# Split fp16 products for the MLP and the query, key and value projections of a fused token, attention and expert layer, and a reordered start

## The reference, cut to what matters

```python
def _L0_tok_ref(x, W1, b1, W2, b2):          # 64 images of 3x224x224 as 196 patches of 768
    h = jax.nn.silu(jnp.einsum('blk,kd->bld', patches, W1) + b1)
    return jnp.einsum('bld,de->ble', h, W2) + b2          # 256 columns

def _L0_attn_ref(x, ...):                    # (64, 228, 256), 16 heads of 16
    xn = _rms_norm(x, ln1_w)
    q, k, v = xn @ Wq, xn @ Wk, xn @ Wv      # then q and k are normalised per head
    attn = (jnp.einsum('bqhd,bkhd->bhqk', q, k) + bias) * scale[None, :, None, None]
    attn = jax.nn.softmax(jnp.where(causal, attn, -1000000.0), axis=-1)
    y = jnp.einsum('bhqk,bkhd->bqhd', attn, v) @ Wo + x
    z = _rms_norm(y, ln2_w)
    return jax.nn.relu(z @ W1) @ W2 + y      # hidden width 1024

def _L0_ffn_ref(x, Wr, W1, b1, W2, b2):      # 8 experts, each takes its top 3648 of 14592 tokens
    h = jax.nn.gelu(jnp.einsum('ekd,edh->ekh', X_in, W1) + b1[:, None, :], approximate=False)
    X_e = jnp.einsum('ekh,ehd->ekd', h, W2) + b2[:, None, :]
    return out.at[idx].add(G * X_e)

h = jnp.concatenate([_L0_tok_ref(x), txt], axis=1)
h = h + _L0_attn_ref(_layernorm(h));  h = h + _L0_ffn_ref(_layernorm(h))
```

## Time and profile before

| | us |
|---|---|
| median of 3 runs | 4300.19 (4299.0 to 4302.61) |
| profiled execution, its own time | 4297.36 |
| its span | 4295.6 |
| mean granted TensorE clock in it | 0.968 of full speed |
| start, up to the second pair's `tok2` block | 175.2 |
| first phase after that (31 passes) | 2492.3 |
| last MLP and router | 54.1 |
| second phase | 1574.0 |

### The profile page before, as it was taken

How to read it: one execution, slowest core, us unless ns; L and a number is a source line. 1 busy time by engine, 2 the same in 40 slices (tenths; PEclk the granted TensorE clock), 3 DMA queues, 4 the chain that set the end, 5 groups by cost and what they waited for, 6 DMA issues and landing times. The chain is left out here.

```text
span 4295.6 us, 78024 instructions
## 1 busy us (share of the span) xinstructions
PE 3876.5 (90%) x26650; PEld 2354.5 (55%) x26650; DVE 2403.7 (56%) x4812; ACT 2035.7 (47%) x3375; POOL 1716.9 (40%) x1367
## 2 busy tenths in 40 slices
PE   2699999999999999999999999339999999999998
PEld 1366566566566566566566566235555555555554
DVE  3455555555555555555555555475555555555554
ACT  1344444444444444444444444225665655655565
POOL 1123323323323323323323322016666666666666
PEclk8799999999999999999999999659999999999999
DMA  7412312312312312312312310532323323323322
GB/s 113 87 35 43 49 34 44 49 34 44 49 34 44 49 34 44 49 34 44 49 34 44 49 22 16 143 99 39 63 45 66 63 46 65 65 46 66 46 46 45
DMA packets 302872, 222.26 MB, mean 52 GB/s; under 512 B 111524, under 2 KB 290182, under 8 KB 302710
## 3 DMA queue, kind: packets, MB, share of 16 engines
q1 hardware_dynamic: 183550, 157.86, 19.1%
q0 software_dynamic: 107264, 62.29, 9.3%
q10 hardware_dynamic: 11896, 0.05, 0.2%
HBM read 117.43 MB, written 63.57 MB: 42 GB/s over the span
## 5 line engine op out<-in xcount | busy, mean ns | idle before, releaser
L1382 DVE TENSOR_TENSOR pr<-pr,bias_t 114x684 f32<-114x684 f32 x512 | 485.6, 968 | 166.3 <-ACT pr L1018 161.9
L1729 POOL DMA_INDIRECT out_dram<-contrib,idx_cur x256 | 531.5, 2076 | 104.8 <-issue 78.8
L1558 DVE SCALAR_TENSOR_TENSOR hTs<-hTe,scales,hTs 128x456 f16<-128x456 f32 x514 | 322.4, 686 | 445.5 <-ACT hTs L1132 445.5
L1018 ACT ACTIVATE pr<-SC 114x684 f32<-114x684 f32 x512 | 376.5, 743 | 339.7 <-PE SC L445 339.4
L511 PE MATMUL G<-w2m,hT 128*114 128x256 f32 x2048 | 511.4, 388 | 1.1 <-DVE hy L1354 1.1
L891 PE MATMUL SC<-xgT,ws 128*128 128x456 f16 x2316 | 468.4, 357 | 0.0
L1722 POOL DMA_INDIRECT xg<-xn_rows,idx_cur x264 | 389.9, 1477 | 117.1 <-issue 60.4
L493 PE MATMUL G<-yT,w1m 128*128 128x456 f32 x1024 | 412.2, 551 | 10.6 <-ACT yT L964 10.6
L371 PE MATMUL G<-img,w1t 128*128 128x392 f32 x768 | 343.4, 538 | 68.3 <-DMA b2t<-in_L_tok_b_dram 49.9
L511 PEld LDWEIGHTS G<-w2m,hT 128*114 128x114 f32 x2048 | 339.9, 178 | 75.6 <-ACT hT L1054 15.4
L1660 POOL TENSOR_TENSOR rstd<-mv,ln_eps 114x4 f32<-114x4 f32 x32 | 7.0, 220 | 881.0 <-DVE mv L1255 881.0
(11 more groups left out here) (229 smaller groups left out, 6725.3 us busy)
## 6 DMA issues: line engine op xcount, KB each, us to landing
raw<-in_x_dram SPq DMA_DIRECT2D x192, 196.0 KB, 6.4
img<-turned SPq DMA_DIRECT2D x384, 98.0 KB, 2.8
we<-in_L_ffn_W_dram SPq DMA_DIRECT2D x34, 1024.0 KB, 7.7
out_dram<-hy SPq DMA_DIRECT2D x32, 456.0 KB
xn_rows<-xn SPq DMA_DIRECT2D x32, 456.0 KB
xg<-xn_rows,idx_cur POOLq DMA_INDIRECT x264, 3.8
out_dram<-contrib,idx_cur POOLq DMA_INDIRECT x256, 5.5
bias_by_distance<-pr SPq DMA_DIRECT2D x1, 3241.9 KB, 37.9
```

Of the source, the lines that this page charges most:

```text
L1018: act.activation(pr[g % 4][:, :, :], SC[g % 2][0:T, :, 0:QW], ACT.Exp).then_inc(exp_done, 1)
L1382: dve.tensor_tensor(pr[g % 4][:, :, :], pr[g % 4][:, :, :], bias_t[:, 2 * pair:2 * pair + 2, :], ALU.mult).then_inc(probs_done, 1)
L1558: dve.scalar_tensor_tensor(hTs[:, 1, m, :], hTe[:, m, :], scale_at(scales, 2, e), hTs[:, 0, m, :], ALU.mult, ALU.subtract).then_inc(h_spli ...
L1729: pool.indirect_dma_start(out=out_rows, out_offset=bass.IndirectOffsetOnAxis(ap=idx_cur[k4][:, t:t + 1], axis=0), in_=contrib[k][:, t, :], ...
```

## The change

1. The projections (`wqkv`), `w1` and `w2` become three fp16 products each. The moving and stationary operands are `xh`, `yh`, `hT` (activations) and `wqkv`, `w1m`, `w2m` (weights), each with a high and a low half in the place of the fp32 data. ScalarE writes the high half; VectorE then writes the low half (`xs_low`, `y2_low`, `hid_low`), and only that frees the bank.
2. Weights are scaled by powers of two from their norms: squares on ScalarE, sums by a TensorE product with ones, exponents on VectorE, then the two halves. For the projections this is done before the first pair, for the MLP after the first pair's attention. The scales are undone where projections are read out and in the residual.
3. `w2` pieces: 8 of 16 stand ahead of the first `qkT`, where it was 2; the rest stand in earlier slots. `mlp_out(0)` stands ahead of `masked_probs`.
4. The bias table is written narrower (341 columns of 455) and read back by three loads. The first images are spread after it, and the table is built ahead of the first `qk_norm`. Loads of the expert biases are moved from ScalarE's queue at the start to SyncE's queue later.
5. In the last pair, the final norm is written by VectorE and all relu are on ScalarE.

On VectorE, in a pass (these rows are the last pass, whose order is that of all), before: from the end of the Newton steps (`rn`) to the low parts of the queries and keys (`qkp`).

The diff, cut to its core:

```diff
@@ operands
-        wqkv = s1("wqkv", [128, KC, 3 * D])
+        wqkv = s1("wqkv", [128, 2, KC, 3 * D], F16)
-        w1m = s1("w1m", [128, KC, HID])
-        w2m = s1("w2m", [128, MC, D])
+        w1m = s1("w1m", [128, 2, KC, HID], F16)
+        w2m = s1("w2m", [128, 2, MC, D], F16)
-        hT = s1("hT", [128, MC, W])
+        hT = s1("hT", [128, 2, MC, W], F16)
...
+        PARTS = ((0, 0), (0, 1), (1, 0))
@@ pe_qkv, pe_w1, pe_w2 (one of three)
+            if m == 0:
+                pe.wait_ge(mlp_split, 2)
-                last = pe.matmul(part.g("w1", m)[:, 0:W], w1m[:, c, m * 128:(m + 1) * 128], yT[:, c, :],
-                                 start=c == 0, stop=c == KC - 1)
+                for n, (wp, yp) in enumerate(PARTS):
+                    last = pe.matmul(part.g("w1", m)[:, 0:W], w1m[:, wp, c, m * 128:(m + 1) * 128], yh[:, yp, c, :],
+                                     start=c == 0 and n == 0, stop=c == KC - 1 and n == len(PARTS) - 1)
@@ slots
-        for n, slot in enumerate((0, 1, 4, 4, 5, 6, 7, 8, 9, 10)):
-            SLOTS[slot].append(("w2", range(6 + n, 7 + n)))
+        for n, slot in enumerate((2, 4, 5, 6)):
+            SLOTS[slot].append(("w2", range(12 + n, 13 + n)))
...
-            w2(0)
+            for n in range(0, 8, 2):
+                w2(n)
             pe_qkT(part, j, 0)
-            w2(2)
+            w2(8)
@@ tensor, start
+            pe.wait_ge(qkv_squares, 2)
+            pe.matmul(SC[1][:, 1, 480:482], sum_ones[:, :], w_sums[:, QK_SUM:V_SUM + 1], start=True, stop=True).then_inc(qkv_norms, 1)
...
+            pe.wait_ge(mlp_squares, 3)
+            pe.matmul(SC[1][:, 1, 484:487], sum_ones[:, :], w_sums[:, WO_SUM:W2_SUM + 1], start=True, stop=True).then_inc(mlp_norms, 1)
@@ scalar
             def relu(part, ms):
                 for m in ms:
                     part.wait_filled(act, "w1", m)
-                    act.activation(hT[:, m, :], part.g("w1", m)[:, 0:W], ACT.Relu).then_inc(evacuated[part.bank("w1", m)], 1)
+                    act.activation(hT[:, 0, m, :], part.g("w1", m)[:, 0:W], ACT.Relu).then_inc(hid_high, 1)
...
             exps(part, 0)
+            act.wait_ge(mlp_folded, 1)
+            squares_of(wo[:, :, :], yT[:, :, 0:D], WO_SUM, mlp_squares)
+            squares_of(flat(w1m_raw), words(w1m), W1_SUM, mlp_squares)
+            squares_of(flat(w2m_raw), words(w2m), W2_SUM, mlp_squares)
+            act.wait_ge(mlp_scale, 1)
+            high_weights(w1m[:, 0, :, :], w1m_raw, W1_K, mlp_high)
+            high_weights(w2m[:, 0, :, :], w2m_raw, W2_K, mlp_high)
@@ vector
+            def xs_low(part, j):
+                for c in range(KC):
+                    dve.wait_ge(xs_high, KC * j + (c + 1))
+                    dve.tensor_tensor(xh[:, 1, c, :], part.g("xsT", c)[:, 0:W], xh[:, 0, c, :],
+                                      ALU.subtract).then_inc(evacuated[part.bank("xsT", c)], 1)
+            def hid_low(part, j, ms):
+                for m in ms:
+                    dve.wait_ge(hid_high, MC * j + (m + 1))
+                    dve.scalar_tensor_tensor(hT[:, 1, m, :], part.g("w1", m)[:, 0:W], 0.0, hT[:, 0, m, :],
+                                             ALU.max, ALU.subtract).then_inc(evacuated[part.bank("w1", m)], 1)
...
             def iteration(part, i):
                 front_a(part, i, False)
                 tail(part, i - 1)
                 router_out(i - 2)
-                front_b(part, i)
+                front_xs(i, range(2))
+                y2_low(part, i - 1)
+                front_xs(i, range(2, NT)).then_inc(xs_done, 1)
+                hid_low(part, i - 1, range(EARLY))
+                xs_low(part, i)
+                hid_low(part, i - 1, (EARLY,))
+                front_xa(part, i)
                 qk_norm(part, i)
+                mlp_out(part, i - 1, 0)
                 masked_probs(part, i)
@@ gpsimd
+            pool.wait_ge(mlp_split, 2)
+            pool.memset(xn2, 0.0).then_inc(xn2_done, 1)
```

More of the change, by code:

```diff
@@ L411, in pe_qkv @@
                         for c in range(KC):
-                            last = pe.matmul(part.g(*key)[0:T, half * D:(half + 1) * D], xsT[:, c, t * T:(t + 1) * T],
-                                             wqkv[:, c, 2 * D:], start=c == 0, stop=c == KC - 1)
+                            for n, (wp, xp) in enumerate(PARTS):
+                                last = pe.matmul(part.g(*key)[0:T, half * D:(half + 1) * D], xh[:, xp, c, t * T:(t + 1) * T],
+                                                 wqkv[:, wp, c, 2 * D:],
+                                                 start=c == 0 and n == 0, stop=c == KC - 1 and n == len(PARTS) - 1)
                 pe_block(part, key, last)
@@ L735, in _ @@
             load_text(1)
+            with nc.allow_non_contiguous_dma(reason="small vectors of weights"):
+                for e in range(NE):
+                    sp.dma_start(fb1c[:, e, :], fb1[e].rearrange("(m p) -> p m", p=128)).then_inc(expert_biases_in, 16)
+                for c in range(KC):
+                    sp.dma_start(fb2c[:, c, :], fb2[:, c * 128:(c + 1) * 128].rearrange("e p -> p e")).then_inc(expert_biases_in, 16)
             def rest(part, i):
@@ L1099, in _ @@
             squares(part)
-            relu(part, range(4))
+            relu(part, range(MC))
             x2_transposed(PAIRS - 1)
@@ L1273, in front_a, with front_xs, front_xa @@
                 stats(h0, mv1, ln1_stats)
-            def front_b(part, j):
+            def front_xs(j, tiles):
                 dve.wait_ge(ln1_scales, j + 1)
-                for t in range(NT):
+                for t in tiles:
                     last = dve.tensor_scalar(xs[:, t, :], h0[:, t, :], mv1[:, t, 0:1], lt[:, 5, t:t + 1],
                                              ALU.subtract, ALU.mult)
-                last.then_inc(xs_done, 1)
+                return last
+            def front_xa(part, j):
                 if part.kind != "first":
@@ L1308, in qk_norm @@
                 step(dve.tensor_tensor(rn[:, :, 0:H], rn[:, :, 0:H], sc_q[:, :, :], ALU.mult))
+                if part.kind != "first":
+                    hid_low(part, j - 1, (4, 5))
                 for t in range(NT):
+                    if part.kind != "first" and t == 2:
+                        hid_low(part, j - 1, (6,))
                     q = qkraw[:, t, :].rearrange("p (h d) -> p h d", d=HD)
@@ L1312, in qk_norm @@
                                       ALU.mult).then_inc(qk_scaled, 1)
+                if part.kind != "first":
+                    hid_low(part, j - 1, (7,))
                 for t in range(NT):
@@ L1420, in _ @@
             router_out(j - 1)
-            relu(part, range(4, MC))
+            y2_low(part, j)
+            hid_low(part, j, range(MC))
             mlp_out(part, j, 0)
@@ L1424, in _ @@
             mlp_stats(part)
+            dve.wait_ge(last_scales, 1)
+            dve.wait_ge(xn2_stored, 16 * (j + 1))
+            for t in range(NT):
+                last = dve.tensor_scalar(xn2[:, t, :], hy[:, t, :], mv2[:, t, 0:1], rstd2[:, t:t + 1],
+                                         ALU.subtract, ALU.mult)
+            last.then_inc(xn2_done, 1)
             router_out(j)
```

216 lines of the change are left out of this document (145 added, 71 removed).

## The result

The changed kernel takes 4330.47 us in the median (4323.89 to 4335.92, 4 runs), the kernel before 4299.59 (4297.12 to 4302.61, 4 runs): ratio 1.0071, 95% interval 1.0053 to 1.0088. It is 0.7% slower; 4194 was forecast, and the range ended at 4262. The profiled execution took 4331.23 us, its span 4329.4.

What follows compares the result with a forecast made beforehand. Taken as bound by TensorE: a pass falls from 80.58 to 77.5 us, so 31 passes give -94.5, start -5, end -7: 4191 from 4297.4, median 4194. The 8-in-10 range was 4100 to 4262.

Steps and rivals of the forecast that it cites:

- TensorE's work: In a pass, fp16 triples replace fp32 products at 0.193, 0.216 and 0.109 us each: -8.8 us if nobody else is late.
- Up to the first `qkT`: In a pass, VectorE's low halves and scaling make the first `qkT` start at 104.3 instead of 102.4: +1.9 us.
- Idle ahead of block 6: In a pass, block 4's low half stands behind the Newton steps, so TensorE idles from 93.3 to 96.2.
- The attention's start: Behind the first `qkT`, 8 `w2` pieces instead of 14 give -6.85 us; waits showing with less filler give +1.3.
- The clock: At the new 2.9 us idle place, clock falls in six passes of ten: +0.6 us a pass (bounds 0 and 1.4).
- the one long idle place: TensorE's new idle 2.9 us ahead of hidden block 6, the place where the forecast put a possible clock fall.
- The rule that I set aside: Skill page's return to half clock in each loop turn: all 31 passes would pay 1.0, sum 12 us higher.
- My rival on the clock: Clock stays low from block 6 until the first `next` product: pass 91.5 us, time 4626; chance 0.06.
- The start: Ahead of the passes: first attention 22 us earlier, MLP split +16.5; together -5 us (from -25 to +15).
- The end: Last pair: `w1` and `w2` pieces save 3.3 us, last norm on VectorE about 2 instead of 4.84: -7 us.
- my signs of being wrong: Wrong if the pass is under 76 or above 79 us, or the patch product starts ahead of 55 us.
- The rival on the loads: fp16 products with 114 columns loaded miss half a record: pass near 88 us, time near 4520; chance 0.03.

Runs made afterwards that it cites:

- tuned_nofill: Changed kernel with y2's low halves ahead of all normalised tiles and `w2` piece 11 moved to attention slot 0, no filling products: 4254.47 us.
- fill_two: Changed kernel with unread fp16 products in two TensorE waits, seven ahead of the first MLP block and fourteen ahead of block 6: 4277.73 us.
- tuned: Changed kernel with y2's low halves ahead of all normalised tiles, `w2` piece 11 in attention slot 0, and 3 and 14 filling products: 4231.43 us.
- fill_w1: Changed kernel with seven unread fp16 products between the last transpose of y2 and the first product of the MLP's first layer: 4311.35 us.
- w2_fp32: Changed kernel with the MLP's second layer left in fp32 in its old slots and no low halves of the hidden layer: 4328.10 us.

## Why the prediction was wrong, by its steps

By the two traces the span grew by 33.8 us: passes +42.5 (29 between the same two events +37.4, the first one's 80.57 to 81.92 +1.3, the last +3.8), start -5.7, end -7.7, and +4.7 in the second phase, which nothing in the change explains; over twenty profiled kernels with the same second phase it took 1571 to 1592 us.

- **TensorE's work** was right: 0.193, 0.22 and 0.11 us a product, and 68.33 us busy in a clean pass without fillers (tuned_nofill) against 76.74 before: -8.4, forecast -8.8. The changed kernel shows only -5.1, since two falls slow its products.
- **Up to the first `qkT`** was right in a clean pass: it starts at 42.95 us of it (fill_two), before 40.86: +2.1, forecast +1.9. Behind a fall it is +3.7.
- **Idle ahead of block 6**: 2.94 us, released by a low half, as forecast.
- **The attention's start** was mis-sized. Forecast -6.85 and +1.3; measured -4.24, so the new waits are 2.6, not 1.3: 0.57, 1.08, 0.35 and 0.80 less the old 0.17. That is 41 us of the 137 by which the passes missed (forecast -94.5, measured +42.5). From the first `next` on another 0.4 us a pass came.
- **The clock** is the step that failed: forecast 0.6 a pass, measured 3.07 (81.92 less 78.85), 2.5 us x 31 = 77 us of those 137. I looked for it at the one long idle place. In the changed kernel that place kept its clock; the two falls stood behind shorter waits, in stretches where TensorE was thinly used (ahead of the second it was busy for 2.1 of 3.4 us), and in 28 of 29 passes. The rows had a sign of it that I read only for its length: ahead of the fall at 156 us in the kernel before there is no long idle place (the longest wait is 1.10 us), only thin use. TensorE is busy there for 2.17 of 4.00 us; the row behind it is in the earlier trace rows:

```profile
152.00:156.00 4.00, 2.17 (x22) 1.05 (x22) 3.31 (x3) 2.19 (x4) 2.86 (x1) 0.96 0.01 4
```

The rule that I set aside was nearer: the Trainium skill, page "TensorE: Matmul & The Clock Gate", section "HAM oscillation — how this bites in real kernels", has the return to half clock paid anew in each turn of a loop that waits between bursts. The trace of the changed kernel agrees (two falls in 28 of 29 passes); that of tuned_nofill does not (none in 18 of 29). The page's own case has waits for DMA; here TensorE waited for VectorE and ScalarE, for 1.39 us and less. My rival on the clock put one huge fall at the wrong place (4626), with nothing between it and 0.6.
- **The start** was right: first attention 22.2 us earlier (forecast 22), then +16.4 for the split (7.8 up to the second pair, 8.6 in its pass; forecast 16.5). Images at 56.7, forecast 61.
- **The end** was right: from the last y2 to the first step of the second phase 46.65 us before, 38.93 after: -7.7, forecast -7.

One of my signs of being wrong came: a pass above 79 (81.94). With the clean pass of 78.85 the kernel would have gained some 53 us on the passes and, by my estimate from the terms above, come out near 4235, inside the range; the forecast's own range began at a gain of 1.5 us a pass, and a clean one has 1.7. The rival on the loads does not follow from its own terms: 77.5 + 4.1 + 8.6 is a pass of 90.2 and not 88. Nothing hangs on it, since the products ran at 0.11 us.

## What to carry to other kernels

When a change shortens TensorE's work but not the chain that feeds it, price the clock at each wait it opens, short ones in thin stretches too, and for every turn of the loop: here two falls ate 3.1 us of a pass of 79. Look at passes one by one: the clean ones tell what the order is worth, the rest what the clock costs. And ask of a split whether TensorE had something better to do in that time; the slower product without the extra halves won, once it stood where the wait was.

## What the runs showed of the hardware

- Products whose result nobody reads can raise speed: 21 of them a pass took 53 us off (4330.5 to 4277.7), and 17 took 23 us off at the same clean pass (tuned_nofill to tuned).
- Falls do not simply follow the longest wait: in the changed kernel a wait of 2.9 us kept 1.00 and one of 1.39 lost it; in tuned_nofill the same waits had a fall in some passes and none in others. Filling one wait can move the fall to another place (fill_w1), and the pattern then repeats over several passes. The two kernels with two falls in 28 of 29 passes, the changed one and w2_fp32, both have passes of 81.92 us, at different orders; why is not shown.
- The same kernel can vary by its falls: fill_two ran from 4248.8 to 4299.7 us in 10 runs, tuned from 4222 to 4233 in 5.
- fp16 products with 114 columns loaded and 256 streamed run 0.11 us apart, with 512 streamed 0.22: no cost of the narrow load shows.
